# A two-layer transformer on one core: finer steps in the order table, side-by-side small matrix products, and weight loads split in two

## The reference

```python
for _ in range(NUM_CYCLES):                       # A and C, 3 cycles
    tf = coupling_net(out)                        # one number a token
    coupling = 0.1 + adaptive_range * (0.7 * gf + 0.3 * tf - 0.5) * 2.0
    out = out + coupling * twist(out)             # [p, -o] of the halves
...
scores = where(causal, q @ k.T * scale, -inf)     # B, 16 heads
...
k_s = k[:, h, ::stride, :]; v_s = v[:, h, ::stride, :]   # E, stride of the head
...
h = relu(s[..., None] * W1 + b1); g = einsum('btmh,mh->btm', h, W2) + b2   # D and F
```

## Time and profile before

| | us |
|---|---|
| median of three runs | 3855.83 (3854.97 to 3858.72) |
| the profiled execution, whole | 3855.25 |
| its span in the trace | 3853.3 |
| PE busy | 3549.4 (92%) |
| DVE busy | 2508.3 (65%) |
| ACT busy | 1839.7 (48%) |
| POOL busy | 955.4 (25%) |

### The profile page before, as it was taken

How to read it: one execution, slowest core, us unless ns; L and a number is a source line. 1 busy time by engine, 2 the same in 40 slices (tenths; PEclk the granted TensorE clock), 3 DMA queues, 4 the chain that set the end, 5 groups by cost and what they waited for, 6 DMA issues and landing times.

```text
span 3853.3 us, 57876 instructions
## 1 busy us (share of the span) xinstructions
PE 3549.4 (92%) x21952; PEld 2062.0 (54%) x21952; DVE 2508.3 (65%) x5003; ACT 1839.7 (48%) x2885; POOL 955.4 (25%) x1030
## 2 busy tenths in 40 slices
...
GB/s 87 1 1 1 1 1 12 1 12 1 1 12 1 12 1 12 1 1 12 1 12 1 12 1 1 12 1 12 1 12 1 7 6 1 12 1 6 1 6 6
DMA packets 39662, 27.26 MB, mean 7 GB/s; under 512 B 18464, under 2 KB 38496, under 8 KB 39392
## 3 DMA queue, kind: packets, MB, share of 16 engines
...
...
## 4 chain that ended last, share of the span: by engine, by line
PE 85%; DVE 7%; ACT 4%; issue 1%; POOL 1%; DMA 0%; DVEq 0%; ACTq 0%; POOLq 0%
PE ps L494 77%; PE ps L505 8%; ACT other L1170 2%; ACT PR L1144 1%; DVE other L859 1%; DVE MX L923 1%; DVE G L961 1%; ACT L1144 1%; DVE MX L917 1%; DVE other L858 0%; DVE XN L948 0%; DVE XT L863 0%; DVE XN L902 0%; DVE XN L899 0%; DVE XN L834 0%
## 5 line engine op out<-in xcount | busy, mean ns | idle before, releaser
L1144 ACT ACTIVATE PR<-ps 128x1024 f32<-128x1024 f32 (+4 forms) x720 | 540.4, 795 | 680.6 <-PE ps L494 677.4
L494 PE MATMUL ps<-MAT 32*128 32x512 f32 (+5 forms) x4928 | 591.1, 490 | 16.4 <-ACT PR L1144 6.1
L923 DVE TENSOR_REDUCE MX<-ps 128x2 f32<-128x1024 f32 (+3 forms) x512 | 392.6, 820 | 272.0 <-PE ps L494 269.2
L1215 POOL TENSOR_TENSOR rstd<-var,neg_half 128x4 f32<-128x4 f32 x144 | 148.3, 1030 | 1216.0 <-DVE var L817 1064.9
L494 PEld LDWEIGHTS ps<-MAT 32*128 32x128 f32 (+2 forms) x4928 | 276.5, 185 | 304.0 <-issue 191.5
L494 PE MATMUL ps<-XT,cn_w 128*128 128x256 f32 x1536 | 367.0, 393 | 4.8 <-DVE XT L861 4.8
L1273 POOL TENSOR_SCALAR_AFFINE_SELECT PR<-PR 128x512 f32<-128x512 f32 x256 | 173.7, 679 | 726.2 <-ACT PR L1144 726.1
L494 PE MATMUL ps<-other,cn_w 128*128 128x512 f32 (+2 forms) x1152 | 324.3, 481 | 12.6 <-ACT other L1061 5.4
L494 PEld LDWEIGHTS ps<-XT,cn_w 128*128 128x128 f32 x1536 | 291.6, 195 | 80.1 <-issue 34.8
L494 PE MATMUL ps<-HI 32*128 32x256 f32 (+4 forms) x3072 | 221.3, 378 | 109.3 <-ACT PR L1144 74.9
L917 DVE TENSOR_REDUCE MX<-ps 128x2 f32<-128x1024 f32 (+6 forms) x256 | 220.3, 903 | 155.4 <-PE ps L494 154.8
...
## 6 DMA issues: line engine op xcount, KB each, us to landing
...
```

The source lines that it names most:

```text
L494: return pe.matmul(dst, lhsT, rhs, start=start, stop=stop, skip_group_check=True)
L923: last = dve.tensor_reduce(MX[:, t, at], src[:, :, a:a + nk[pair]], AX_X, ALU.max)
L1144: freed(act.activation(PR[0:m, tile_of((s, q, g, kt)), 2 * pair:2 * pair + 2, q0:T], ps[0:m, b:b + 2, 0:T - q0], ACT.Exp, scale=SCALE[s]), ...
L1215: pool.tensor_tensor(rstd[:, c, :], var[:, c, :], neg_half[:], ALU.pow).then_inc(rstd_ready.sem, 1)
```

## The change

Seven things are changed together.

1. The table. It is written anew, begins at another point of the turn, and has two new kinds of step: `mix.S.k.v` (VectorE's mixing of half v in cycle k, so far part of `tf`) and `relu.S.i` (two of the eight relu readouts on ScalarE and two of the running sums on VectorE, so far part of `inner`).
2. Mixing. `ZT` is gone. ScalarE turns the tanh of `tf` into the whole coupling factor (two more activations of 128x256 a cycle), and VectorE does four plain products and sums of 128x256 for each half.
3. The causal mask is 32x32 pieces: eight small products where two of 128x128 stood, in four row strips and four column strips of the array.
4. `KVT` is 128 partitions by 256 tokens, the two halves of the tokens above each other. The content keys of B are two products of 64 rows by 256 tokens, one in each half of the array, and the values alternate between the halves. Two transposes are left of four.
5. In E all key tiles of a head take every fourth key (or every `s`-th beyond stride 4), so that heads of stride 1, 2 and 4 share their first key tile; the values are 12 products. The stationary operands of `exp.E` and `v.E` are read with the steps that follow from it.
6. `latent`, `proj`, `att`, `content.E` and the content queries of B take single banks in place of pairs.
7. Loading. The first block issues the first sequence and the 20 loads that stage A needs, and does not wait for them; the other loads go out in the second block, behind the second sequence. VectorE prepares its constants in two parts, ahead of the first `h1` and ahead of the first `latent`; GpSimd sets most of its constants in the second block.

```diff
 TURN = """
...
-1:h3.A.0 0:sum.B.3.1 0:sum.B.3.2 0:exp.B.3.3 1:tf.A.0 -1:exp.E.3.0 0:sum.B.3.3 1:h1.A.1 -1:content.E.1 1:h2.A.1
...
+1:tf.A.1 -1:max.E.1.1 1:mix.A.1.0 0:proj.B -1:exp.E.2.0 1:mix.A.1.1 0:stats.C 1:h1.A.2 0:normal.C -1:content.E.0
...
+def tile_of_keys(columns, step, stride, t):
+    if stride > 4:
+        return columns[:, ::stride // step]
+    return columns[:, (0, 2, 1, 3)[t] // step::4 // step]
...
+        V_PARTS = [(0, 10, 4, 0), (10, 14, 8, 0), (14, 16, 16, 0)] + [
+            (E_SLOT[t], E_SLOT[t] + sum(n > t for n in e_tiles), 1, t) for t in range(1, TT)]
...
             def _(sp):
-                for dst, src in loads:
-                    sp.dma_start(dst, src, allow_slow_non_contiguous=True).then_inc(loaded, 16)
...
-                sp.wait_ge(loaded, ALL_LOADS)
+                sp.dma_start(X[:, 0], x_v[0]).then_inc(x_loaded[0], 16)
+                for dst, src in first_loads:
+                    sp.dma_start(dst, src, allow_slow_non_contiguous=True).then_inc(loaded_first, 16)
...
+                    if s == "B":
+                        product(single_bank(), ("content", s, q, g, "q"), [(w_qdec[:, g, :], QL[:, q % 2, :])])
+                        b = pair_bank()
+                        dst = take(b, "content", s, q, g, "k", width=2)
+                        for v in range(2):
+                            half = slice(64 * v, 64 * v + 64)
+                            last = mm(dst[:, v, 0:T // 2], w_kdec[half, g, :], KVT[half, q % 2, :])
+                        last.then_inc(full[b], 1)
+                        return
...
                     if s == "B":
                         for pair in (0, 1):
                             for t, first, nk in rounds:
-                                for n in range(2):
-                                    at = first[pair] + t * P
-                                    last = mm(dst[pair][:, n, at:at + P], ident_b[:], mask_q[:], False, True)
+                                at = first[pair] + t * P
+                                for b in range(4):
+                                    for n in range(2):
+                                        row = slice(ROWS * (2 * pair + n), ROWS * (2 * pair + n + 1))
+                                        last = mm(dst[pair][ROWS * b:ROWS * b + ROWS, n, at:at + P], ident_b[row, row],
+                                                  mask_q[row, b, :], False, True)
...
+                def mixed(s, q, k, v):
...
+                    dve.wait_ge(coupling_ready.sem, coupling_ready.at(s, q, k, v))
+                    tok = slice(v * T // 2, (v + 1) * T // 2)
+                    dve.tensor_tensor(WT[:, a, tok], TF[:, a, tok], XT[:, c, 1, tok], ALU.mult)
+                    link(dve.tensor_tensor(TF[:, a, tok], TF[:, a, tok], XT[:, c, 0, tok], ALU.mult))
+                    dve.tensor_tensor(XT[:, c, 0, tok], XT[:, c, 0, tok], WT[:, a, tok], ALU.add).then_inc(first_moved.sem, 1)
+                    dve.tensor_tensor(XT[:, c, 1, tok], XT[:, c, 1, tok], TF[:, a, tok],
+                                      ALU.subtract).then_inc(second_moved.sem, 1)
...
+                    for v in range(2):
+                        read_out(act, "tf", s, q, k, v)
+                        own = TF[:, area_of[s], v * T // 2:(v + 1) * T // 2]
+                        act.activation(own, own, ACT.Identity, scale=c_tf,
+                                       bias=gc_h[:, q % CH, 3:4]).then_inc(coupling_ready.sem, 1)
...
-                def inner(s, q):
+                def inner(s, q, i):
                     src = when_full(act, "s", s, q)
-                    for j in range(8):
+                    for j in (2 * i, 2 * i + 1):
```

More of the change, by code:

```diff
@@ L41 @@
--1:max.E.0.1 0:h1.C.0 1:back.A 1:stats.B -1:exp.E.1.0 -1:sum.E.2.0 -1:exp.E.1.1 1:normal.B 0:h2.C.0 -1:max.E.0.2
--1:sum.E.1.0 -1:divide.E.2 1:xt.B -1:max.E.0.3 0:h3.C.0 1:latent.B -1:shift.E.0 -1:sum.E.1.1 -1:exp.E.0.0 1:kvt.B
-1:turn.B.0.k 1:turn.B.0.q -1:exp.E.0.1 -1:sum.E.0.0 0:tf.C.0 1:content.B.0 -1:sum.E.0.1 -1:exp.E.0.2 -1:exp.E.0.3
--1:divide.E.1 -1:sum.E.0.2 -1:sum.E.0.3 1:max.B.0.0 0:h1.C.1 1:max.B.0.1 -1:divide.E.0 0:h2.C.1 1:max.B.0.2
-1:turn.B.1.k -1:att.E 1:shift.B.0 1:v.B 0:h3.C.1 1:exp.B.0.0 1:turn.B.1.q 0:tf.C.1 1:content.B.1 -1:proj.E
@@ L46 @@
-1:sum.B.0.0 -1:stats.E2 1:exp.B.0.1 0:h1.C.2 -1:normal.E2 1:max.B.1.0 0:h2.C.2 -1:xt.E2 1:sum.B.0.1 0:h3.C.2
-1:max.B.1.1 -1:up.0 0:tf.C.2 1:exp.B.0.2 -1:up.1 -1:up.2 1:max.B.1.2 0:back.C -1:up.3 1:exp.B.0.3 0:stats.D -1:up.4
-1:turn.B.2.k 1:shift.B.1
+1:tf.A.1 -1:max.E.1.1 1:mix.A.1.0 0:proj.B -1:exp.E.2.0 1:mix.A.1.1 0:stats.C 1:h1.A.2 0:normal.C -1:content.E.0
+1:h2.A.2 -1:shift.E.1 -1:max.E.0.0 1:h3.A.2 -1:divide.E.3 0:xt.C -1:max.E.0.1 1:tf.A.2 1:mix.A.2.0 1:mix.A.2.1
+-1:sum.E.2.0 -1:max.E.0.2 0:h1.C.0 1:back.A 1:stats.B -1:exp.E.1.0 0:h2.C.0 -1:max.E.0.3 -1:sum.E.1.0 0:h3.C.0
@@ new lines @@
+1:normal.B -1:exp.E.1.1 -1:shift.E.0 -1:divide.E.2 1:xt.B -1:exp.E.0.0 -1:sum.E.1.1 1:latent.B -1:exp.E.0.1 0:tf.C.0
+1:turn.B.0.k -1:sum.E.0.0 -1:exp.E.0.2 -1:sum.E.0.1 1:kvt.B 0:mix.C.0.0 1:turn.B.0.q -1:exp.E.0.3 0:mix.C.0.1
+1:content.B.0 0:h1.C.1 1:max.B.0.0 -1:divide.E.1 0:h2.C.1 -1:sum.E.0.2 1:max.B.0.1 0:h3.C.1 -1:sum.E.0.3 0:tf.C.1
+1:max.B.0.2 1:turn.B.1.k -1:divide.E.0 1:shift.B.0 1:v.B 1:turn.B.1.q 1:content.B.1 0:mix.C.1.0 -1:att.E 0:mix.C.1.1
+1:exp.B.0.0 -1:proj.E 1:exp.B.0.1 -1:stats.E2 0:h1.C.2 -1:normal.E2 1:max.B.1.0 1:sum.B.0.0 0:h2.C.2 -1:xt.E2
@@ new lines @@
+1:sum.B.0.1 0:h3.C.2 1:max.B.1.1 0:tf.C.2 -1:up.0 0:mix.C.2.0 1:exp.B.0.2 -1:up.1 0:mix.C.2.1 -1:up.2 1:exp.B.0.3
+1:sum.B.0.2 0:back.C 1:max.B.1.2 1:turn.B.2.k 1:shift.B.1 1:turn.B.2.q -1:up.3 1:exp.B.1.0 -1:up.4 0:stats.D
+0:normal.D 1:content.B.2 -1:up.5 -1:up.6 1:max.B.2.0 0:xt.D -1:up.7 1:max.B.2.1 1:sum.B.0.3 0:inner.D 1:max.B.2.2
+0:relu.D.0 1:divide.B.0 0:relu.D.1 0:relu.D.2 0:relu.D.3 -1:down.0 -1:down.1 1:sum.B.1.0 -1:centre 1:exp.B.1.1
+1:shift.B.2 1:exp.B.1.2 1:sum.B.1.1 -1:scale 1:exp.B.1.3 -1:stats.F 1:turn.B.3.k 1:sum.B.1.2 1:sum.B.1.3 0:mout.D
@@ new lines @@
+1:exp.B.2.0 -1:normal.F 1:turn.B.3.q 0:stats.E -1:xt.F 1:exp.B.2.1 -1:inner.F 0:normal.E -1:relu.F.0 1:sum.B.2.0
+-1:relu.F.1 1:exp.B.2.2 1:content.B.3 -1:relu.F.2 1:sum.B.2.1 1:exp.B.2.3 -1:relu.F.3 1:max.B.3.0 0:xt.E -1:mout.F
+1:sum.B.2.2 1:max.B.3.1 0:v.E 1:max.B.3.2 0:content.E.3 1:shift.B.3 1:divide.B.1 2:stats.A 2:normal.A 1:sum.B.2.3
+1:exp.B.3.0 0:content.E.2 1:exp.B.3.1 1:sum.B.3.0 1:divide.B.2 2:xt.A 1:exp.B.3.2 2:h1.A.0 1:sum.B.3.1 1:exp.B.3.3
+2:h2.A.0 0:max.E.3.0 1:sum.B.3.2 1:sum.B.3.3 2:h3.A.0 0:shift.E.3 0:max.E.2.0 2:tf.A.0 2:mix.A.0.0 0:content.E.1
@@ L49 @@
+0:exp.E.3.0 2:mix.A.0.1 1:divide.B.3 2:h1.A.1 0:shift.E.2 0:max.E.1.0 2:h2.A.1 1:att.B 2:h3.A.1 0:sum.E.3.0
 """
@@ L1125, in values @@
+                    for first, end, m in ((0, 10, P), (10, 14, 64), (14, 16, 32), (16, E_SLOTS, P)):
+                        last = act.activation(VE[0:m, first:end, 0:HD], src[0:m, first:end, :], ACT.Copy)
                     freed(last, "v", s, q, 0)
```

380 lines of the change are left out of this document (188 added, 192 removed).

## The result

The changed kernel takes 3830.73 us (median of four runs, 3826.0 to 3832.26) against 3855.4 for the kernel before beside it: a ratio of 0.9934, 95% interval 0.9917 to 0.9951. Forecast were 3755 and a range that ends at 3830. The direction was right, the size a quarter of the forecast.

The account below looks back on a forecast made before the run. PE (TensorE) work was taken as the bound, busy 3549.4 of 3853.3 us; -4.0 us a turn over 15 turns (-60) and the start's -39 took 3855.25 to 3756, rounded to 3755 us, range 3685 to 3830.

Parts of the forecast that it names:

- The start: Loading before PE's first product: PE starts 42 us earlier, +3 for the longer coupling chain, so -39.
- The work of a turn: PE's products: content keys -1.7, values of B -0.8, latent -0.2, E 0 and +0.3, mask -1.3, array part changes +1.7.
- the exponentials of E: Keys of `exp.E`, now read with steps of several tokens: +0.3 us a turn.
- The mask's pieces: Causal mask in `max.B`: 256 pieces a turn at 0.009 us each, 2.3 us, so -1.3 (-1.8 to +3.8).
- dear: Rival on the mask: each piece costs 0.029 us, +5.1 us a turn, 3831 us; chance 0.14.
- unshared: Rival on the mask: pieces run one behind the other at 0.056 us, +12.0 a turn, 3935 us; chance 0.06.
- the lower bound: Mask: sixteen pieces side by side take 0.056 + 15 x 0.004 us, 0.007 each, 1.8 us a turn.
- The values of E: Twelve instructions fewer, but sixteen loads with a step of four tokens: 4.7 us against 4.86, taken as 0.
- The waits of a turn: PE's waits, mainly at `max.B.3.0`: four short ones, -0.9; clock -1.6, waits elsewhere +0.5; together -2.0 (-7 to +2.5).
- Waits move: Rival: ScalarE's relus among content and score readouts hold up other banks, +2.5 rather than -2.0, 3823 us; chance 0.10.
- The clock: Behind PE's long wait at `max.B.3.0`: 1.6 us a turn lost at granted clock 0.59 is taken back.
- The ends: Filling and draining of the pipeline: 15 turns of savings counted, one left off because savings there fall into waits.

Follow-up runs that it names:

- e2: The changed kernel with the step table of the kernel before, its products, mask, start and mixing kept: 3826.5 us.
- e4: The changed kernel with GpSimd's two additions behind `xt.E` working on a quarter of the tokens only: 3779.1 us (0.9807).
- e1: The changed kernel with two table steps moved, `normal.E` behind `relu.F.3` and `xt.E` behind `sum.B.2.2`: 3777.0 us (0.9807).
- e3: The changed kernel with the causal mask as before, two products of 128x128 instead of eight small ones: 3827.8 us.
- e11: e9 with the causal mask as two products of 128x128: 3730.6 us.
- e9: The changed kernel with three table steps moved (`xt.F`, `normal.E`, now between `relu.F.1` and `relu.F.2`, and `sum.B.2.2`): 3731.0 us (0.9672).
- e12: e9 with the two products of `up.1` done twice, 1.72 us more TensorE work a turn: 3739.9 us.
- e15: e9 with `up.1` and `up.2` taking only the first half of the features, 1.72 us less work a turn: 3701.2 us.
- e8: e2 with `latent`, `proj`, `att`, the content of E and the content queries of B in pairs of banks again: 3811.6 us.

## Why the prediction was wrong

**The start** was right: -42 forecast, -40.6 to the first product; from there to the first values of B it took 4.7 us longer, where +3 was taken for the longer coupling chain; in e2, with the same chain in the old table, it is 3.5. Start and chain -35.9 against -39.

**The work of a turn** was right in its parts, nearly. Content keys 0.63 a group from start to start where 1.00 was (a turn's mean, not the 1.05 of one row), so -1.5 for -1.7; values of B 1.06, -0.9 for -0.8; latent -0.2 as forecast; the exponentials of E, for which no row stood behind the +0.3, came to +0.4. The mask's pieces cost 0.011 to 0.013 each where I had chosen 0.009, and the old ones 4.4 us a turn rather than 3.6, so -1.5 for -1.3; they are neither dear nor unshared. The 0.004 us a piece in the lower bound stood in no row either. The values of E cost 5.06, not 4.7, and 0.3 more than before where I took 0: sixteen loads in steps of four take 3.9 us, 0.24 each, as the earlier trace rows had said, but the eight narrow ones more than I gave them. This row of the changed kernel is the weight load (us, mean ns):

```profile
L468 PEld LDWEIGHTS ps<-w_v,XT 128*128 128x128 f32 x16 | 3.9, 327 | 0.1
```

Most of the difference is the banks: in `exp.B.0.1` the kernel before lost 1.7 us waiting for a pair that VectorE's addition of the projection (L948) held. From its first row to the next step's it took 3.21 us where the changed kernel takes 1.52, and only 0.16 of that shows as idle time; I had priced the single banks at nothing.

```profile
1430.52 1.56 PE L494 MATMUL ps<-MAT 32*128 32x384 f32 x8
1432.24 1.56 PE L494 MATMUL ps<-MAT 32*128 32x384 f32 x8 [0.16 <-DVE XN L948]
1433.73 3.72 PE L494 MATMUL ps<-XT,cn_w 128*128 128x256 f32 x16
```

**The waits of a turn** are the step that failed. I walked ScalarE's list against PE's and got 3.6 us in four pieces; 1.8 in three pieces came. But the readouts have a consumer, and I did not walk its list: on VectorE `normal.E` had come between `inner.F` and the first sum, and GpSimd's two additions, which start when PE reaches `xt.E`, had come beside the sums. Both were in the order of the changed kernel. Idle time rose by 4.9 us where I took -0.4: a wait of 6.65 us at `mout.F` was not in my walk. e4, with the additions made small, and e1, which moves both causes out of the way, give 52 to 54 us back. "Waits move" was a rival at 0.10, but with ScalarE as its cause and +2.5 as its price; its 3823 came near the time by luck.

**The clock** failed with it: I gave back 1.6 us because no wait would be long; it took 1.1 more (1.5 over thirteen turns). And 1.6 was not all that the kernel before lost there. The window behind that of the earlier trace rows has a granted clock of 0.74, so 13 x 0.26 = 3.4 us, which the forecast did not count:

```profile
1299.00:1312.00 13.00, 12.89 (x114) 9.38 (x114) 5.83 (x11) 1.33 (x7) 3.32 (x2) 0.74 0.29 82
```

**Adding up** failed as a method, beyond its terms. 1.5 us of the mask (in e3 and e11), 2.3 us of waits in e9 and 1.72 us of work in e12 each moved the turn by less than 0.1 us, while 1.72 us less in e15 moved it by 2.2. A sum of small terms over 15 turns says little where the time at the lower clock can make up the difference; a forecast should have had this in its range.

**The ends** gave 28 us, where I had counted two turns' worth, 8. It is the table (31 us between e2 and the changed kernel), and it hid most of the 39 us by which the thirteen full turns are longer.

What the mixing costs or gives by itself was not tried apart from the products; e2 and e8 hold it together with them.
